# One kernel, last layer: the order of TensorE's products in the expert retrieval, the last turn of each chunk, the stores at the end, and who builds one-hots

## The chip, the cores and the metric

The kernel runs on one core of one Trainium2 chip. The metric is the device time of one execution in microseconds (us). Engines are named PE (TensorE), DVE (VectorE), ACT (ScalarE), POOL (GpSimd) and SP (SyncE).

## The reference

The network has four layers, each a gated "cross attention" and a gated feed-forward part, on x of 8 x 256 rows (2048 rows) of 512 features. The change lies in the very last part only, the fourth feed-forward:

```
q = (x @ Wq).reshape(b, t, H, 2, DK)                 # H = 4 heads
sim1, sim2 = products of the halves of q with the keys
s1, i1 = top_k(sim1, 8); s2, i2 = top_k(sim2, 8)
final_scores, pk_idx = top_k(all 64 sums, 8)         # 8 experts for each head and row
w_down, w_up = e_down[final_indices], e_up[final_indices]
hidden = silu(einsum('btd,bthkd->bthk', x, w_down)) * relu(final_scores)
out = einsum('bthk,bthkd->btd', hidden, w_up)
x = x + tanh(g_ffn[3]) * out
```

Each row has 32 chosen experts out of 4096, each with its weight. x is layer-normalised before it goes in.

## The kernel before

X stays in SBUF as 16 tiles of 128 rows. Earlier phases have left the chosen indices (`first`, `second`, transposed, and `idx`), the weights (`first[:, 1, :]`, `wts`) and the transposed x in DRAM (`xT_dram`). The phase `retrieve_phase` then does two things side by side.

Eleven tiles (TG = 11) go the dense way. They are cut into three chunks of 3, 4 and 4 tiles (NQ = 3), and for each chunk all 4096 experts are gone through in 32 blocks of 128 (EB = 32), two blocks to a turn (`k`, NP = 16 turns). Buffers come in pairs, one for an even block (h = 0) and one for an odd block (h = 1). For a block n:

- SP loads the 256 KB of down and the 256 KB of up rows. ACT rounds each to a high part (`down_high`, `up_high`), DVE takes the rest (`down_low`, `up_low`).
- `hidden` on PE (line 2610): 12 matmuls (4 pieces of the features, three products of high and low parts) give 128 experts by up to 512 rows in `h_ps[h]`.
- The chain of a block, which alternates between two engines: ACT `silu` (L2666), DVE `weight`, a product with the block of G (L2762), ACT `high` (L2671), DVE `low` (L2766).
- `add_up` on PE (line 2622): three matmuls of 512 columns for each tile of the chunk, 9 or 12, add to one accumulator `o_ps[a]` for each tile. `begin` (L2601) zeroes the accumulators, `end` (L2627) closes them.

G holds the weight of every expert for every row. It is made by products of one-hots, `weigh` on PE (L2594; 4 products, seen as 8 records): `oh2` from DVE, `oh1` from DVE (L2753) or from ACT (`one_hot`: an Abs, L2684, and a Relu, L2687, for each of the 4 columns that it takes), and ACT copies the result to G (`keep`, L2678). There are 88 groups: the first 24 (N0) are made in a loop ahead of chunk 0 (the head), where DVE alone builds the one-hots; the other 64 are made inside the turns of chunks 0 and 1, where ACT builds 3 of 4 (chunk 0) or 4 of 4 (chunk 1) of `oh1`.

PE's order in a turn of blocks n and n+1 is: hidden(n), hidden(n+1), weigh, add_up(n), weigh, add_up(n+1). Between chunks ACT rounds the next chunk's x (`xh`, L2735) and DVE takes its rest (`split_x`, L2772), after the last turn; PE waits for `xl_ready`. DVE adds the sums to X tile by tile (L2853) once `end` has closed all accumulators; `begin` of the next chunk waits for that.

Five tiles (NG = 5) go by gathering: POOL fetches for each of 160 lists of 128 rows the down and the up rows with indirect DMAs (L2554), DVE makes a dot product (L2788) and an addition (L2802) of each. These pairs are spread over the turns by `pairs_in`: 3 or 4 slots to a turn, 52, 64 and 56 to a chunk (172 in all); the addition of a list runs 12 slots behind its dot product.

All waits are semaphores, all orders are written out by hand, and every engine works strictly in its own order. At the end POOL stores the gathered tiles in one transfer (1280 KB) and the last chunk in one transfer (1024 KB).

Of the kernel before, what the change touches and what calls it, by code (L numbers as in the profile page):

```python
# [2469 lines left out]
def retrieve_phase(nc, R, A, name, xT_dram, rows_dram, first, second, idx, wts, stat, gate, out):  # L2470
# [48 lines left out]
    summed, y_ready, stored = ph.sem("summed"), ph.sem("y"), ph.sem("stored")  # L2519
# [9 lines left out]
    @block.sync  # L2529
    def _(sp):  # L2530
        def load_down(n, h):
            sp.wait_ge(edl_ready, n + 1)
            sp.dma_start(ed[h][:, :, :], A["L3_ffn_e_down"][bass.ds(n % EB, 1)].rearrange("e p c k -> p (e c) k")).then_inc(ed_in[h], 16)

        def load_up(n, h):
            sp.wait_ge(eul_ready, n + 1)
            sp.dma_start(eu[h][:, :], A["L3_ffn_e_up"][bass.ds(n % EB, 1)].rearrange("e p c -> p (e c)")).then_inc(eu_in[h], 16)

        load_up(0, 0)
        load_down(0, 0)  # L2540
        load_down(1, 1)
        load_up(1, 1)
        with sp.Fori(1, NQ * NP) as i:
            load_down(2 * i, 0)
            load_down(2 * i + 1, 1)
            load_up(2 * i, 0)
            load_up(2 * i + 1, 1)

    @block.gpsimd
    def _(pool):  # L2550
# [13 lines left out]
        for q in range(NQ):  # L2564
            for k in range(NP):
                if k == 1 and q < NQ - 1:
                    pool.wait_ge(xl_ready, DC * (q + 1))
                    pool.dma_start(xc[:, :, :], xT_dram[q + 1]).then_inc(xc_in, 16)
                if k == 2 and q:
                    pool.wait_ge(y_ready, begun[q])  # L2570
                    pool.dma_start(out[begun[q - 1] * P:begun[q] * P, :].rearrange("(a p) c -> p a c", p=P), X[:, begun[q - 1]:begun[q], :]).then_inc(stored, 16)
                for j in pairs_in[q, k]:
                    if j + ND < NU:
                        gather(rows_dram[:, :], gd, gd_in, dotted, j + ND)
                    if LAG <= j < NU + LAG - ND:
                        gather(up_rows, gu, gu_in, added, j - LAG + ND)
        pool.wait_ge(added, NU)
        pool.dma_start(out[TG * P:N, :].rearrange("(a p) c -> p a c", p=P), X[:, TG:NT, :]).then_inc(stored, 16)
        pool.wait_ge(y_ready, TG)
        pool.dma_start(out[begun[-1] * P:TG * P, :].rearrange("(a p) c -> p a c", p=P), X[:, begun[-1]:TG, :]).then_inc(stored, 16)  # L2580
# [3 lines left out]
    def _(pe):  # L2584
# [18 lines left out]
        def hidden(n, q):  # L2603
            cols = tiles[q] * P
            for h in range(2):
                pe.wait_ge(edl_ready, n + h + 3)
                pe.wait_ge(sl_ready, n + h + 1)
                for c in range(DC):
                    for m, (w, x) in enumerate(((edh, xh), (edh, xl), (edl, xh))):
                        last = pe.matmul(h_ps[h][:, 0:cols], lhsT=w[h][:, c, :], rhs=x[:, c, 0:cols],  # L2610
                                         start=(c == 0 and m == 0), stop=(c == DC - 1 and m == 2))
                last.then_inc(h_ready, 1)

        def add_up(n, q, more, late=True):
            for h in range(2):
                if more:
                    weigh(n + h + N0, h, n + h - 1 if late else None)
                pe.wait_ge(eul_ready, n + h + 3)
                pe.wait_ge(atl_ready, n + h + 3)
                for a in range(tiles[q]):  # L2620
                    for w, x in ((ath, euh), (ath, eul), (atl, euh)):
                        last = pe.matmul(o_ps[a][:, :], lhsT=w[h][:, a * P:(a + 1) * P], rhs=x[h][:, :], start=False, stop=False)  # L2622
                last.then_inc(used, 1)

        def end(q):
            for a in range(tiles[q]):
                last = pe.matmul(o_ps[a][:, :], lhsT=zero[:, :], rhs=zero[:, 0:1].to_broadcast([P, D]), start=False, stop=True)  # L2627
            last.then_inc(summed, 1)

        pe.wait_ge(zeroed, 1)  # L2630
        with pe.Fori(0, N0 // 2) as i:
            for h in range(2):
                weigh(2 * i + h, h)
        for q in range(NQ):
            pe.wait_ge(xl_ready, DC * (q + 1))
            hidden(q * EB, q)
            begin(q)
            add_up(q * EB, q, q < NQ - 1, q > 0)
            built = min(NP, max(1, (NO - N0 - q * EB) // 2))
            if built > 1:  # L2640
                with pe.Fori(1, built) as k:
                    hidden(q * EB + 2 * k, q)
                    add_up(q * EB + 2 * k, q, True)
            if built < NP:
                with pe.Fori(built, NP) as k:
                    hidden(q * EB + 2 * k, q)
                    add_up(q * EB + 2 * k, q, False)
            end(q)

    @block.scalar  # L2650
    def _(act):
# [46 lines left out]

        def turn(q, k, more):
# [8 lines left out]
            high(n + 1, 1, cols)  # L2708
            held, build = n + N0 < NO, n + N0 + 2 < NO
# [4 lines left out]
            if build:  # L2714
                one_hot(n + N0 + 2, 0, q)
# [4 lines left out]
            if build:  # L2720
                one_hot(n + N0 + 3, 1, q)
# [8 lines left out]
        down_high(1, 1)  # L2730
        for q in range(NQ):
            act.wait_ge(xc_in, 16 * q + 16)
            act.wait_ge(h_ready, q * EB + 2)
            for c in range(DC):
                act.activation(xh[:, c, 0:tiles[q] * P], xc[:, c, 0:tiles[q] * P], ACT.Copy).then_inc(xh_ready, 1)  # L2735
# [8 lines left out]
    def _(dve):  # L2744
# [65 lines left out]
        def turn(q, k, more, ahead):  # L2810
# [140 lines left out]
```

## Time and profile before

| | us |
|---|---|
| median of 3 runs | 1713.95 (1712.74 to 1713.96) |
| the profiled execution, as timed | 1718.21 |
| its span, first to last instruction | 1716.5 |
| PE busy / DVE busy / ACT busy over the span | 1370.1 / 1419.7 / 937.7 |
| the head of the retrieval (weights' loop) | about 1061 to 1105.3 |
| chunk 0, 1, 2 | 1105.3 to 1282.3, to 1502.3, to 1708.3 |

Times in rows are microseconds from the span's start. A row of the timeline has the start, the length, engine, line, operation, what is written from what is read, how many instructions are merged in it, and in brackets the idle time of the engine just before it and what ended it. Matmuls overlap one another, so their spacing is read from their starts, not from their lengths. "remote" stands where a signal ended a wait and the profile shows no instruction ending at that time; "issue" where it shows no signal.

### The profile page before, as it was taken

Reading aid. Unit: us, or ns where it says so; the run is one execution under the profiler, and the core shown is the slowest. Engines: PE = TensorE matmul, PEld = TensorE weight load, DVE = VectorE, ACT = ScalarE, POOL = GpSimd, SP = SyncE. Lnnn points to the kernel's source line nnn. Section 1 sums busy time; section 2 is a strip of 40 time slices with the busy share of each in tenths; the row PEclk is TensorE's granted clock in tenths of the full one; section 3 lists DMA queues with packets and bytes.
Section 4 is the critical chain, followed back from the end, with each engine's and each line's share of the span. In section 5 each row is a group of like instructions: output and inputs, shape, how many; then the busy total and the mean of one; then the engine's idle time right before and its main releaser. Section 6 shows DMA issues by size and latency. Waiting matters only on the chain. (4 is left out here: it accounts for less than half of the span.)

```text
span 1716.5 us, 23588 instructions
## 1 busy us (share of the span) xinstructions
PE 1370.1 (80%) x6594; PEld 1019.2 (59%) x6614; DVE 1419.7 (83%) x3057; ACT 937.7 (55%) x1967; POOL 545.1 (32%) x607
## 2 busy tenths in 40 slices
PE   3888548886999668466675981799989999989987
PEld 2444324445788533344524881699878788867766
DVE  5999868975887698798499998989888799977775
ACT  3467746652333272675434442488787788833332
POOL 0000025553110000000033224147666577746542
PEclk8899879997999866687876995999999999989999
DMA  6230020000000120464100003178887888877774
GB/s 217 92 126 13 1 80 0 0 1 1 1 1 1 46 104 1 150 206 135 56 1 19 25 26 95 49 211 256 230 240 224 229 249 241 255 208 238 220 212 143
DMA packets 92338, 197.44 MB, mean 115 GB/s; under 512 B 16040, under 2 KB 25896, under 8 KB 91488
## 3 DMA queue, kind: packets, MB, share of 16 engines
q0 software_dynamic: 27168, 90.98, 18.9%
q1 hardware_dynamic: 65088, 105.56, 18.7%
q8 instruction: 28, 0.46, 0.1%
q14 instruction: 54, 0.44, 0.1%
HBM read 181.04 MB, written 15.47 MB: 114 GB/s over the span
## 5 line engine op out<-in xcount | busy, mean ns | idle before, releaser
L2554 POOL DMA_INDIRECT L3f_gd<-rows,idx x160 | 188.5, 1178 | 192.9 <-DVE L3f_gd L2788 160.8
L2554 POOL DMA_INDIRECT L3f_gu<-in_L_ffn_e_up,idx x160 | 178.5, 1116 | 73.7 <-issue 46.3
L2622 PE MATMUL L3f_o_ps<-L3f_euh,L3f_ath 128*128 128x512 f32 x352 | 148.2, 421 | 27.1 <-DVE L3f_atl L2766 23.9
L2610 PE MATMUL L3f_h_ps<-L3f_xh,L3f_edh 128*128 128x512 f32 (+1 forms) x384 | 145.1, 378 | 9.1 <-DVE L3f_xl L2772 5.8
L2610 PE MATMUL L3f_h_ps<-L3f_xl,L3f_edh 128*128 128x512 f32 (+1 forms) x384 | 144.4, 376 | 0.0
L2610 PE MATMUL L3f_h_ps<-L3f_xh,L3f_edl 128*128 128x512 f32 (+1 forms) x384 | 144.3, 376 | 0.0
L2622 PE MATMUL L3f_o_ps<-L3f_euh,L3f_atl 128*128 128x512 f32 x352 | 140.2, 398 | 0.0
L2622 PE MATMUL L3f_o_ps<-L3f_eul,L3f_ath 128*128 128x512 f32 x352 | 139.8, 397 | 0.0
L2594 PE MATMUL L3f_g_ps<-L3f_oh 128*128 128x128 f32 x704 | 99.0, 286 | 46.4 <-DVE L3f_oh L2753 40.9
L2762 DVE TENSOR_TENSOR L3f_at<-L3f_at,L3f_G 128x512 f32<-128x512 f32 (+1 forms) x96 | 62.1, 647 | 80.3 <-ACT L3f_at L2666 51.2
L2594 PEld LDWEIGHTS L3f_g_ps<-L3f_oh 128*128 128x128 f32 x704 | 94.4, 200 | 55.0 <-issue 46.2
L2666 ACT ACTIVATE L3f_at<-L3f_h_ps 128x512 f32<-128x512 f32 (+1 forms) x96 | 53.5, 557 | 131.3 <-PE L3f_h_ps L2610 62.9
L2802 DVE SCALAR_TENSOR_TENSOR X<-L3f_gu,L3f_coef,X 128x512 f32<-128x512 f32 x160 | 119.5, 747 | 1.0
L2788 DVE SCALAR_TENSOR_TENSOR L3f_gd<-L3f_gd,L3f_xs 128x512 f32<-128x512 f32 x160 | 109.9, 687 | 0.0
L2622 PEld LDWEIGHTS L3f_o_ps<-L3f_euh,L3f_ath 128*128 128x128 f32 x352 | 67.7, 192 | 50.8 <-issue 39.1
L2687 ACT ACTIVATE L3f_oh<-L3f_oh,first,L3f_minus 128x128 f32<-128x128 f32 x216 | 90.2, 486 | 2.1
L2610 PEld LDWEIGHTS L3f_h_ps<-L3f_xh,L3f_edh 128*128 128x128 f32 x384 | 73.3, 191 | 21.1 <-DVE L3f_xl L2772 6.3
L2671 ACT ACTIVATE L3f_ath<-L3f_at 128x512 fp32r<-128x512 f32 (+1 forms) x96 | 57.4, 598 | 50.8 <-DVE L3f_at L2762 29.8
L333 PE MATMUL L0x_vp_ps<-L0x_W,L0x_V 128*128 128x512 f32 x128 | 66.8, 671 | 19.1 <-ACT L0x_sv L493 19.1
L2610 PEld LDWEIGHTS L3f_h_ps<-L3f_xl,L3f_edh 128*128 128x128 f32 x384 | 73.4, 191 | 10.9
L2610 PEld LDWEIGHTS L3f_h_ps<-L3f_xh,L3f_edl 128*128 128x128 f32 x384 | 73.2, 191 | 10.5
L1034 POOL TENSOR_TENSOR L0f_s<-L0f_s,L0f_su 128x1 f32<-128x1 f32 x16 | 5.4, 337 | 231.5 <-DVE L0f_s L1123 231.5
(595 smaller groups left out, 3755.8 us busy)
## 6 DMA issues: line engine op xcount, KB each, us to landing
L3f_eu<-in_L_ffn_e_up SPq DMA_DIRECT2D x96, 256.0 KB
L3f_ed<-in_L_ffn_e_down SPq DMA_DIRECT2D x96, 256.0 KB
L2x_ed<-in_L_ffn_e_down SPq DMA_DIRECT2D x32, 256.0 KB, 3.4
rows<-L2x_eo SPq DMA_DIRECT2D x32, 256.0 KB, 2.4
wgu<-in_L_ffn_w_gate_upT SPq DMA_DIRECT2D x4, 1408.0 KB, 7.9
X<-in_x SPq DMA_DIRECT2D x4, 1024.0 KB, 10.1
L0x_V<-in_ctxT SPq DMA_DIRECT2D x8, 512.0 KB, 3.8
L1f_C<-in_ctx SPq DMA_DIRECT2D x2, 2048.0 KB, 13.1
```

What stands on the lines that cost most here:

```text
L333: last = pe.matmul(vp_ps[:, :], lhsT=V[b % 3][:, c, j * P:(j + 1) * P], rhs=W[:, c, D:2 * D], start=(c == 0), stop=(c == DC - 1))
L1034: pool.tensor_tensor(at(s, n, 2), at(s, n, 0), at(su, n), ALU.mult).then_inc(sx_ready, 1)
L2554: pool.indirect_dma_start(buf[j % ND][:, :], None, table, bass.IndirectOffsetOnAxis(ap=idx[:, j:j + 1], axis=0)).then_inc(sem[j % ND], 16)
L2594: last = pe.matmul(g_ps[h][:, g, :], lhsT=oh2[h][:, g, :], rhs=oh1[h][:, g, :], start=True, stop=True)
L2610: last = pe.matmul(h_ps[h][:, 0:cols], lhsT=w[h][:, c, :], rhs=x[:, c, 0:cols], start=(c == 0 and m == 0), stop=(c == DC - 1 and m == 2))
L2622: last = pe.matmul(o_ps[a][:, :], lhsT=w[h][:, a * P:(a + 1) * P], rhs=x[h][:, :], start=False, stop=False)
L2666: act.activation(at[h][:, 0:cols], h_ps[h][:, 0:cols], ACT.Silu).then_inc(sl_ready, 1)
L2671: act.activation(ath[h][:, 0:cols], at[h][:, 0:cols], ACT.Copy).then_inc(ath_ready, 1)
L2687: last = act.activation(oh1[h][:, g, :], oh1[h][:, g, :], ACT.Relu, scale=minus[:, n * GR + g:n * GR + g + 1], bias=first[:, 1, n * GR + g ...
L2762: dve.tensor_tensor(ah, ah, Ge, ALU.mult).then_inc(at_ready, 1)
L2788: dve.scalar_tensor_tensor(gd[j % ND][:, :], gd[j % ND][:, :], 1.0, xs[:, j // S, :], ALU.mult, ALU.mult, accum_out=hid[:, j:j + 1]).then_ ...
L2802: dve.scalar_tensor_tensor(X[:, TG + j // S, :], gu[j % ND][:, :], coef[:, j:j + 1], X[:, TG + j // S, :], ALU.mult, ALU.add).then_inc(add ...
```

## The change

1. Products alternate. PE's order becomes hidden(n+1), weigh, add_up(n), weigh, hidden(n+2), add_up(n+1): each hidden product is issued one add_up earlier than before. hidden(n) of a chunk's first block stands ahead of the loop, and the last turn of a chunk has no hidden(n+2).
2. The split of the next chunk's x moves into the last turn: on ACT behind `high` of block n+1, on DVE behind `low` of block n+1.
3. The accumulators are closed tile by tile, each right behind the last add_up of its tile, and each closing signals; DVE's addition to X waits for its own tile only.
4. The last chunk is stored by SP, each tile when it is done; the gathered tiles are stored as 4 tiles once those are done and 1 tile at the end.
5. In the head ACT builds 1 of the 4 `oh1` of a group (from group 4 on, 22 groups), DVE 3 of 4. ACT's loop over the 24 groups is written out.

```diff
+    GH, HW = 1, 4
+    HB = N0 + 2 - HW
+    def far_before(done):
+        return HB * GH + GA[0] * min(done, EB) + GA[1] * max(done - EB, 0)
 @block.sync
+        for a in range(begun[-1], TG):
+            sp.wait_ge(y_ready, a + 1)
+            sp.dma_start(out[a * P:(a + 1) * P, :], X[:, a, :]).then_inc(out_last, 16)
+        sp.wait_ge(out_last, 16 * tiles[-1])
 @block.gpsimd
+        pool.wait_ge(added, NU - S)
+        pool.dma_start(out[TG * P:N - P, :]..., X[:, TG:NT - 1, :]).then_inc(stored, 16)
         pool.wait_ge(added, NU)
-        pool.dma_start(out[TG * P:N, :]..., X[:, TG:NT, :]).then_inc(stored, 16)
-        pool.wait_ge(y_ready, TG)
-        pool.dma_start(out[begun[-1] * P:TG * P, :]..., X[:, begun[-1]:TG, :]).then_inc(stored, 16)
+        pool.dma_start(out[N - P:N, :], X[:, NT - 1, :]).then_inc(stored, 16)
 @block.tensor
+        def add_up(n, h, q, closing=False):
...
+                if closing:
+                    pe.matmul(o_ps[a][:, :], lhsT=zero[:, :], rhs=..., start=False, stop=True).then_inc(summed, 1)
+        def turn(n, q, more, ahead=HB, first=False, last=False):
+            hidden(n + 1, 1, q)
+            if first:
+                begin(q)
+            if more:
+                weigh(n + N0, 0, ahead - 1)
+            add_up(n, 0, q)
+            if more:
+                weigh(n + 1 + N0, 1, ahead)
+            if not last:
+                hidden(n + 2, 0, q)
+            add_up(n + 1, 1, q, last)
 @block.scalar
+        def high_x(q):
+            act.wait_ge(xc_in, 16 * q + 16)
+            act.wait_ge(h_ready, q * EB + 2)
+            for c in range(DC):
+                act.activation(xh[:, c, 0:tiles[q] * P], xc[...], ACT.Copy).then_inc(xh_ready, 1)
 turn:       high(n + 1, 1, cols)
+            if k == NP - 1 and q < NQ - 1:
+                high_x(q + 1)
+                for n in range(N0):
+                    keep(n, 0, n // 2, n % 2)
+                    if n + 2 >= HW:
+                        one_hot(n + 2, n % 2, GH, GH * (n + 2 - HW))
 @block.vector
 turn:       low(n + 1, 1, cols)
+            if k == NP - 1 and q < NQ - 1:
+                split_x(q + 1)
-        with dve.Fori(2, N0 // 2 + 1) as i:
+        with dve.Fori(HW // 2, N0 // 2 + 1) as i:
             for h in range(2):
-                one_hots(2 * i + h, h)
+                one_hots(2 * i + h, h, GH)
-            if q < NQ - 1:
-                split_x(q + 1)
-            dve.wait_ge(summed, q + 1)
             for a in range(tiles[q]):
+                dve.wait_ge(summed, begun[q] + a + 1)
                 dve.scalar_tensor_tensor(X[:, begun[q] + a, :], o_ps[a][:, :], tg..., X..., ALU.mult, ALU.add).then_inc(y_ready, 1)
```

## Rows read from the trace of the kernel before

**Rows 1.** Page, part 1: busy us, share of the span, instructions of each engine.
```profile
PE 1370.1 (80%) x6594; PEld 1019.2 (59%) x6614; DVE 1419.7 (83%) x3057; ACT 937.7 (55%) x1967; POOL 545.1 (32%) x607
```
**Rows 2.** Windows over chunks 0, 1, 2: us, busy by engine, clock, DMA share, GB/s.
```profile
1105.30:1282.30 177.00, 168.31 (x935) 153.23 (x935) 158.79 (x342) 146.91 (x356) 107.72 (x88) 0.98 0.76 225
1282.30:1502.30 220.00, 210.07 (x1031) 176.79 (x1032) 191.56 (x373) 179.65 (x421) 149.20 (x133) 0.97 0.82 240
1502.30:1708.30 206.00, 188.12 (x775) 145.50 (x776) 151.58 (x288) 72.77 (x131) 99.10 (x96) 0.98 0.69 203
```
**Rows 3.** Timeline of PE, first matmuls of hidden blocks in chunks 0, 1, 2.
```profile
1116.17 0.33 PE L2610 MATMUL L3f_h_ps<-L3f_xh,L3f_edh 128*128 128x384 f32 x1
...
1126.30 0.34 PE L2610 MATMUL L3f_h_ps<-L3f_xh,L3f_edh 128*128 128x384 f32 x1
...
1304.06 0.39 PE L2610 MATMUL L3f_h_ps<-L3f_xh,L3f_edh 128*128 128x512 f32 x1
...
1306.78 0.39 PE L2610 MATMUL L3f_h_ps<-L3f_xh,L3f_edh 128*128 128x512 f32 x1
...
1316.75 0.39 PE L2610 MATMUL L3f_h_ps<-L3f_xh,L3f_edh 128*128 128x512 f32 x1
...
1520.39 0.39 PE L2610 MATMUL L3f_h_ps<-L3f_xh,L3f_edh 128*128 128x512 f32 x1
...
1695.86 0.39 PE L2610 MATMUL L3f_h_ps<-L3f_xh,L3f_edh 128*128 128x512 f32 x1
```
**Rows 4.** Windows over single turns: two of chunk 0, two of chunk 2.
```profile
1150.40:1160.60 10.20, 10.12 (x59) 9.18 (x58) 10.11 (x22) 9.00 (x23) 7.55 (x7) 1.00 0.71 230
1181.10:1192.30 11.20, 11.20 (x66) 10.41 (x65) 11.20 (x25) 9.62 (x23) 8.84 (x8) 1.00 0.84 260
...
1639.30:1651.10 11.80, 11.38 (x50) 8.84 (x49) 10.22 (x20) 4.65 (x9) 5.97 (x6) 1.00 0.82 227
1664.80:1676.70 11.90, 11.48 (x50) 8.93 (x49) 9.09 (x17) 4.73 (x10) 4.47 (x4) 1.00 0.54 163
```
**Rows 5.** Timeline of ACT and PE, waits inside chunks 1 and 2.
```profile
1349.94 0.60 ACT L2666 ACTIVATE L3f_at<-L3f_h_ps 128x512 f32<-128x512 f32 x1 [5.15 <-remote]
...
1352.80 0.77 PE L2622 MATMUL L3f_o_ps<-L3f_euh,L3f_ath 128*128 128x512 f32 x1 [4.00 <-DVE L3f_atl L2766]
...
1567.04 0.47 PE L2622 MATMUL L3f_o_ps<-L3f_euh,L3f_ath 128*128 128x512 f32 x1 [2.19 <-DVE L3f_atl L2766]
```
**Rows 6.** Timeline of DVE in the head, two groups in a row.
```profile
1102.51 0.74 DVE L2749 TENSOR_TENSOR L3f_oh<-ident,second 128x512 f32<-128x512 f32 x1
...
1103.11 1.17 DVE L2753 TENSOR_SCALAR L3f_oh<-ident,first 128x128 f32<-128x128 f32 x4
...
1104.13 0.75 DVE L2749 TENSOR_TENSOR L3f_oh<-ident,second 128x512 f32<-128x512 f32 x1
```
**Rows 7.** Timeline of ACT in chunk 1: keep, and one-hots of one group.
```profile
1297.98 0.58 ACT L2678 ACTIVATE L3f_G<-L3f_g_ps 128x512 f32<-128x512 f32 x1
...
1298.98 1.27 ACT L2684 ACTIVATE L3f_oh<-ident,first 128x128 f32<-128x128 f32 x4
1300.28 1.65 ACT L2687 ACTIVATE L3f_oh<-L3f_oh,first,L3f_minus 128x128 f32<-128x128 f32 x4
```
**Rows 8.** Timeline of PE and DVE at the two joints between chunks.
```profile
1288.06 0.80 PE L2610 MATMUL L3f_h_ps<-L3f_xh,L3f_edh 128*128 128x512 f32 x1 [5.80 <-DVE L3f_xl L2772]
...
1294.02 0.69 DVE L2762 TENSOR_TENSOR L3f_at<-L3f_at,L3f_G 128x512 f32<-128x512 f32 x1 [4.03 <-ACT L3f_at L2666]
...
1511.75 0.69 DVE L2762 TENSOR_TENSOR L3f_at<-L3f_at,L3f_G 128x512 f32<-128x512 f32 x1 [3.64 <-ACT L3f_at L2666]
```
**Rows 9.** Timeline of DVE and POOL at the end of the span.
```profile
1708.29 2.73 DVE L2853 SCALAR_TENSOR_TENSOR X<-L3f_o_ps,tg,X 128x512 f32<-128x512 f32 x4 [2.56 <-PE L3f_o_ps L2627]
...
1711.31 0.81 POOL L2580 DMA_DIRECT2D out<-X  x1 [4.36 <-DVE X L2853]
```
**Rows 10.** Page, part 6, an earlier store of 256 KB: KB, us to landing.
```profile
rows<-L2x_eo SPq DMA_DIRECT2D x32, 256.0 KB, 2.4
```

More of the change, by code:

```diff
@@ L2576, in _ @@
                         gather(up_rows, gu, gu_in, added, j - LAG + ND)
+        pool.wait_ge(added, NU - S)
+        pool.dma_start(out[TG * P:N - P, :].rearrange("(a p) c -> p a c", p=P), X[:, TG:NT - 1, :]).then_inc(stored, 16)
         pool.wait_ge(added, NU)
-        pool.dma_start(out[TG * P:N, :].rearrange("(a p) c -> p a c", p=P), X[:, TG:NT, :]).then_inc(stored, 16)
-        pool.wait_ge(y_ready, TG)
-        pool.dma_start(out[begun[-1] * P:TG * P, :].rearrange("(a p) c -> p a c", p=P), X[:, begun[-1]:TG, :]).then_inc(stored, 16)
+        pool.dma_start(out[N - P:N, :], X[:, NT - 1, :]).then_inc(stored, 16)
         pool.wait_ge(stored, 16 * (NQ + 1))
@@ L2601, in begin, with hidden @@
                 pe.matmul(o_ps[a][:, :], lhsT=zero[:, :], rhs=zero[:, 0:1].to_broadcast([P, D]), start=True, stop=False)
-        def hidden(n, q):
+        def hidden(n, h, q):
             cols = tiles[q] * P
-            for h in range(2):
[L2606 to L2633, printed above, removed]
+            pe.wait_ge(edl_ready, n + 3)
+            pe.wait_ge(sl_ready, n + 1)
+            for c in range(DC):
+                for m, (w, x) in enumerate(((edh, xh), (edh, xl), (edl, xh))):
+                    last = pe.matmul(h_ps[h][:, 0:cols], lhsT=w[h][:, c, :], rhs=x[:, c, 0:cols],
+                                     start=(c == 0 and m == 0), stop=(c == DC - 1 and m == 2))
@@ new lines, in hidden @@
+            last.then_inc(h_ready, 1)
+        def add_up(n, h, q, closing=False):
+            pe.wait_ge(eul_ready, n + 3)
+            pe.wait_ge(atl_ready, n + 3)
+            for a in range(tiles[q]):
+                for w, x in ((ath, euh), (ath, eul), (atl, euh)):
+                    last = pe.matmul(o_ps[a][:, :], lhsT=w[h][:, a * P:(a + 1) * P], rhs=x[h][:, :], start=False, stop=False)
+                if closing:
+                    pe.matmul(o_ps[a][:, :], lhsT=zero[:, :], rhs=zero[:, 0:1].to_broadcast([P, D]), start=False, stop=True).then_inc(summed, 1)
+            last.then_inc(used, 1)
@@ new lines, in turn @@
+        def turn(n, q, more, ahead=HB, first=False, last=False):
[10 more added lines that the diff above has]
+            add_up(n + 1, 1, q, last)
+        pe.wait_ge(zeroed, 1)
+        for n in range(HW):
+            weigh(n, n % 2)
@@ L2634, in _ @@
+        with pe.Fori(HW // 2, N0 // 2) as i:
+            for h in range(2):
+                weigh(2 * i + h, h, 2 * i + h - HW + 1)
         for q in range(NQ):
             pe.wait_ge(xl_ready, DC * (q + 1))
[L2636 to L2648, printed above, removed]
+            n = q * EB
+            hidden(n, 0, q)
+            turn(n, q, q < NQ - 1, n + HB if q else HB, first=True)
+            with pe.Fori(1, NP - 1) as k:
+                turn(n + 2 * k, q, q < NQ - 1, n + 2 * k + HB)
+            turn(n + 2 * NP - 2, q, q < NQ - 1, n + 2 * NP - 2 + HB, last=True)
@@ L2678, in keep, with one_hot @@
             act.activation(Gs, g_ps[h][:, :, :].rearrange("p g (a e) -> p a e g", a=4), ACT.Copy).then_inc(G_ready, 1)
-        def one_hot(n, h, q):
-            done = n - N0 - 2
+        def one_hot(n, h, given, far):
             act.wait_ge(g_ready, n + 1)
-            for g in range(GA[q]):
+            for g in range(given):
                 act.activation(oh1[h][:, g, :], io[:, :], ACT.Abs, scale=-1.0, bias=first[:, 0, n * GR + g:n * GR + g + 1]).then_inc(far_ready, 1)
-            act.wait_ge(far_ready, GA[0] * min(done + 1, EB) + GA[1] * max(done + 1 - EB, 0))
-            for g in range(GA[q]):
+            act.wait_ge(far_ready, far + given)
+            for g in range(given):
                 last = act.activation(oh1[h][:, g, :], oh1[h][:, g, :], ACT.Relu, scale=minus[:, n * GR + g:n * GR + g + 1],
@@ L2697, in hidden_units @@
                     act.activation(act_hid[:, g], hid[:, g], ACT.Silu).then_inc(hid_ready, 1)
+        def high_x(q):
+            act.wait_ge(xc_in, 16 * q + 16)
+            act.wait_ge(h_ready, q * EB + 2)
+            for c in range(DC):
+                act.activation(xh[:, c, 0:tiles[q] * P], xc[:, c, 0:tiles[q] * P], ACT.Copy).then_inc(xh_ready, 1)
         def turn(q, k, more):
@@ L2730, in _ @@
         down_high(1, 1)
+        high_x(0)
         for q in range(NQ):
[L2732 to L2735, printed above, removed]
             if q == 0:
-                with act.Fori(0, N0 // 2) as i:
-                    for h in range(2):
-                        keep(2 * i + h, 0, i, h)
+                for n in range(N0):
+                    keep(n, 0, n // 2, n % 2)
+                    if n + 2 >= HW:
+                        one_hot(n + 2, n % 2, GH, GH * (n + 2 - HW))
             for k in range(NP):
```

6 lines of the change are left out of this document (3 added, 3 removed).

## The prediction

> **What bounds the kernel now.** I read the page first, then windows, then the timeline. The page has PE at 80% and DVE at 83% of the span [rows 1]: two engines close together, so the limit has to be read stage by stage. The windows over the three chunks of the retrieval [rows 2], 603 us of 1716.5, are all that this change touches beside the head and the end. In chunk 0 PE is busy 168.3 of 177 us, DVE 158.8; in chunk 1 210.1 and 191.6 of 220; in chunk 2 188.1 and 151.6 of 206. PE's busy time counts overlapping ends, so I take its true need from starts. In chunk 0 an undisturbed turn goes from 1116.17 to 1126.30, 10.13 us; in chunk 1 from 1304.06 to 1316.75, 12.69 us, its 12 hidden matmuls taking 1306.78 - 1304.06 = 2.72 us, 0.227 each [rows 3]. A turn of chunk 2 has no `weigh`: 48 matmuls of 512 columns at 0.227 are 10.9 us. Really it takes (1695.86 - 1520.39) / 14 = 12.53 us [rows 3]. So the largest slack of PE lies in chunk 2, some 1.6 us in each turn.
>
> DVE's need: in chunk 0 it is busy for 10.11 of 10.20 us in a turn with three gathered pairs and 11.20 of 11.20 in one with four [rows 4]; with every fourth turn of the long kind that is 10.4 a turn, over PE's 10.13. Chunk 0 is bound by DVE from about its fifth turn. In chunk 2 DVE needs 10.2 or 9.1 [rows 4], mean 9.7, under PE's 10.9.
>
> What stalls PE inside the chunks is the chain silu, weight, high, low between a hidden product and its add_up. The before order leaves a block of h = 0 one hidden product (and in chunks 0 and 1 one `weigh`) of cover. The worst place shows it: ACT's silu waited 5.15 us, until 1349.94, for a signal that the profile gives to no instruction ending then ("remote"), and PE then stood 4.00 us before 1352.80 [rows 5]. PE's signal simply came late. Smaller ones of this kind cost chunk 2 about 2 us in about every second turn, as the 2.19 before 1567.04 [rows 5]. At the joints between chunks PE stands 5.80 us for the split of x, and DVE in turn 4.03 and 3.64 us for PE [rows 8].
>
> **The change part by part.** The sum is made against the profiled execution, 1718.21 us (span 1716.5 and 1.7 around it), which is 4.3 above the median of 1713.95.
>
> *Head.* DVE sets the pace, one group from 1102.51 to 1104.13, 1.62 us, of which the four tensor_scalar take 1.02 by their starts, 0.255 each [rows 6]. One of the four goes to ACT: DVE then needs 1.37. ACT needs a keep (0.58), an Abs and a Relu of one column; four of them go in 1.27 and 1.65 [rows 7], about 0.32 and 0.42 each, and a wait on its own signal between, some 1.4 together. So the period is about 1.4, ACT and DVE level, and 22 groups save 22 x 0.2 = 4.4. From both sides: 0, if the waits between ACT and PE do not overlap, to 22 x 0.25 = 5.5. I take 4; writing out the loop I cost at nothing, since ACT's instructions in the turns are written out already.
>
> *Chunk 0, alternating.* Four turns at PE's 10.13, twelve at DVE's 10.4, and 1.4 for opening and closing the accumulators make 167 of the 177 now [rows 2]. At most 10 can be won. But where DVE is the bound it lags, PE waits for add_up(n), and the extra cover is already spent: of a late signal of 3 to 4 us only part is absorbed. I take 4.5, bounds 0 and 10.
>
> *Joint 0 to 1.* The split costs DVE what it did (four subtractions, no new ones) but stands ahead of PE's last add_up instead of behind all gathers. hidden(n+2) then finds xl ready; PE waits next at `begin`, since the additions to X still stand behind a `down_low`, an `up_low`, two one-hots and three gathered pairs on DVE. DVE no longer waits its 4.03 us [rows 8], and what it does afterwards comes earlier by that. With the first turn's matmuls, which now run at the low level of the clock after the pause (the granted clock was 0.97 over the chunk [rows 2]), I take 5. *Joint 1 to 2*: 3.64 [rows 8] of DVE and about 1 of PE, 4.5. Bounds of both together: 6, if a new wait at `begin` lets the clock fall again, and 11.
>
> *Chunk 1.* At 12.69 us a turn PE has nothing left to win: alternating costs and gives nothing there. What goes is part of the one disturbance, 4.00 us and then a few us of slow matmuls (the first after it is 0.77 long, where others are 0.39 [rows 3, 5]). One more add_up of 12 matmuls, 2.7 us, stands between hidden(n) and add_up(n) now, so of the late 5.15 some 1.5 remain and the clock may stay up. I take 5, bounds 0 and 6.5.
>
> *Chunk 2, the largest term.* Cover for h = 0 grows from 2.7 to 5.4 us, and for h = 1 likewise from 2.7 (an add_up) to 5.4, against a chain of 2.86 (silu at 1349.94 to add_up at 1352.80 [rows 5]). But a new order of waits appears: hidden(n+1) now runs behind add_up(n-1), so its signal comes 5.4 us after hidden(n)'s end instead of 2.7, and `weight` of n+1 stands on DVE ahead of all gathers. Follow DVE: from `weight` of n+1 at +6.0, the remaining work of its turn (9.7 less 2.4 for weight, down_low, low and up_low) ends at +13.3, which is +2.4 in the next turn's time; `low` ends 2.1 later at +4.5; PE wants it at +5.4. So the loop closes with 1 us to spare at PE's 10.9, 0.3 in turns with four pairs. Late signals of 2 us in every second turn eat that: about 11.35 a turn. (12.53 - 11.35) x 15 = 17.7; I take 17.5. Bounds: 24 at 10.9, and 7 if only the small waits of the chain (0.2 to 0.5 us a turn) go.
>
> The same balance for chunk 1: DVE's turn of 11.7 closes its loop at 11.9, under 12.69; for chunk 0 at 10.05, under 10.4. ACT's hidden order is fine in all: high, keep and one-hots follow signals that come no later in the turn.
>
> *End.* DVE's four additions (2.73 us) end at 1711.0, POOL issues at 1711.31 [rows 9], and the span ends at 1716.5, 5.2 later. Now three of the four additions lie beside the last matmuls, the last ends about 1709.1, and a store of 256 KB on SP lands after 2.4 [rows 10]; with some 1.2 behind the landing, an estimate (5.2 less 2.4 and the longer transfer of 1024 KB), that is 1712.9. I take 3.5, bounds 1.5 and 4.7. The store of the gathered tiles is hidden by PE's last turn either way.
>
> Sum: 4 + 4.5 + 5 + 4.5 + 5 + 17.5 + 3.5 = 44. 1718.2 - 44 = 1674.2 profiled, less 4.3 for the median: **1670**.
>
> **The rivals.** *(A) Late signals stay late.* Their lateness on h = 1 goes straight into DVE, which has 1 us to spare in chunk 2 and none in chunk 0. Then chunk 0 gives 0, chunk 1 2, chunk 2 7, and with 4 + 9.5 + 3.5 the gain is 26: 1688. For it: DVE is busy in 11.20 of 11.20 us in long turns [rows 4]. Against: in chunk 2 DVE has over 1 us a turn.
>
> *(B) All is absorbed.* Head 4, chunk 0 9, joints 10, chunk 1 6, chunk 2 24, end 4 give 57: 1657. It needs signals that are late only because PE was disturbed itself.
>
> *(C) Slower.* If PE's signals come late because PE runs without a pause, the new order, which takes its pauses away, makes every signal of h = 1 late. In its place, `weight` of n+1, DVE then idles: with a delay of 2 us each turn, chunk 0 closes at 12.05 (against 11.0 now), chunk 1 at 12.9 to 13.8 (12.69), chunk 2 at 12.85 (12.53). That costs 17 + 13 + 5 = 35 against 17.5 from joints, head and end: 1731. It decides from about 1.2 us of delay in every turn. For it: late signals stand in stages of full PE. Against: chunk 1 took 220 us [rows 2], which is 16 turns at 12.69 (203), one such disturbance and the joint, so most of its turns, though PE never pauses in them, have none.
>
> *(D) The clock falls.* The granted clock is 0.97 or 0.98 in all three chunks [rows 2]. If PE, waiting briefly for DVE in more places, ran at 0.90, its 570 us of matmuls would grow by 8%, 45 us, and eat the gain: 1715. The Trainium skill, "TensorE: Matmul & The Clock Gate", section "A second HAM failure mode: psum-queue depth-cycling", says that a PE that pauses often and briefly between groups, as it moves from one accumulator bank to the next, can swing between its two clock levels. That speaks against finer alternation; the trace disagrees so far, with 1.00 in four single turns that have such pauses and bank changes [rows 4], so by the page the time would be this rival's, by the rows the forecast's.
>
> *(E) Nothing changes*, because DVE goes through its work in the old order and PE's new order only moves its waits: the joints, the head and the end would still be there, so this is (A) at least. Only if the early hidden(n+2) waited for `down_low` would it not do what it says; DVE does that second in its turn, some 6 us before.
>
> **How the numbers follow.** Forecast 0.60 (1662 to 1680), A 0.20, B 0.10, C 0.05, D and others 0.05. A comparison of this kernel can tell about 0.2%, 3.4 us. Faster 0.92, within 0.2% 0.02, slower 0.06. The range: the sum of upper bounds (5.5 + 10 + 11 + 6.5 + 24 + 4.7 = 62) ends at 1652, which needs all at once, so 1655; above, A with 4 us on it, 1692.
>
> **What would show it.** PE's hidden starts in chunk 2 about 11.3 us apart, no bracket over 1 us before L2622 in most turns; chunk 1 at 12.69 as before; no wait for L2772 at the joints, one of 1 to 3 us at `begin`; a head period of 1.4 us; the last store issued near 2 us after PE's last matmul. The prediction is wrong if chunk 2's turn stays above 12, or if chunk 1's leaves 12.69, or if DVE shows waits for silu before `weight` of the odd block that add up to more than it lost before.

## The result and the profile after

The changed kernel took 1673.67 us in the median (1671.16 to 1676.94) beside 1713.35 us for the kernel before: a ratio of 0.9775, 95% interval 0.9752 to 0.9798. The forecast was 1670 in 1655 to 1692. The profiled execution took 1676.94 us with a span of 1675.2; against 1716.5 the span is 41.3 us shorter. These runs, with the kernel before's, are called the first measurement below.

The windows over the three chunks of the changed kernel, in the columns of [rows 2] (us, busy by engine, clock, DMA share, GB/s):

```profile
1101.90:1273.20 171.30, 165.76 (x936) 151.27 (x937) 158.17 (x339) 147.62 (x356) 107.58 (x87) 1.00 0.77 232
1273.20:1483.40 210.20, 207.02 (x1032) 174.28 (x1033) 192.26 (x374) 178.01 (x423) 145.73 (x131) 0.99 0.85 251
1483.40:1671.90 188.50, 180.26 (x775) 144.55 (x774) 152.30 (x289) 73.63 (x131) 102.27 (x99) 0.99 0.77 228
```

Each chunk is shorter (177.0, 220.0 and 206.0 before), DVE is as busy in each as before to within 0.8 us, and the granted clock rose from 0.97 or 0.98 to 0.99 or 1.00. In the kernel before, six stretches of 3.4 or 6.8 us inside this time ran at a granted clock of 0.5, the level of 1.2 GHz, each at or just behind a pause of PE; in the changed kernel two of 3.4 us are left, at 1281.1 and 1540.6. Two windows of the kernel before, in the same columns:

```profile
1286.00:1292.80 6.80, 4.74 (x11) 3.77 (x12) 3.99 (x7) 0.06 (x1) 2.87 (x3) 0.50 0.66 196
1350.90:1357.70 6.80, 4.90 (x12) 3.88 (x13) 6.67 (x13) 5.57 (x14) 2.36 (x2) 0.50 0.67 184
```

For the sums below I cut the time at PE's own events, the same in every trace: the head (first `weigh` to first hidden), chunk 0 (to its last closing), joint (from there to the next chunk's first add_up), and so on. In us, both profiled in the first measurement:

| | before | after | won | forecast |
|---|---|---|---|---|
| ahead of the head | 1061.1 | 1059.4 | 1.7 | 0 |
| head | 44.3 | 42.5 | 1.8 | 4 |
| chunk 0 | 176.9 | 171.3 | 5.6 | 4.5 |
| joint 0 to 1 | 15.3 | 11.3 | 4.0 | 5 |
| chunk 1 | 204.6 | 198.9 | 5.7 | 5 |
| joint 1 to 2 | 12.3 | 7.3 | 5.0 | 4.5 |
| chunk 2 | 193.8 | 181.3 | 12.5 | 17.5 |
| end | 8.2 | 3.3 | 4.9 | 3.5 |

PE's starts of hidden blocks in the changed kernel, one and the same place of a turn in each pair, answer to [rows 3]:

```profile
1114.86 0.33 PE L2620 MATMUL L3f_h_ps<-L3f_xh,L3f_edh 128*128 128x384 f32 x1
1124.99 0.33 PE L2620 MATMUL L3f_h_ps<-L3f_xh,L3f_edh 128*128 128x384 f32 x1
...
1293.69 0.39 PE L2620 MATMUL L3f_h_ps<-L3f_xh,L3f_edh 128*128 128x512 f32 x1
1306.38 0.39 PE L2620 MATMUL L3f_h_ps<-L3f_xh,L3f_edh 128*128 128x512 f32 x1
...
1498.91 0.39 PE L2620 MATMUL L3f_h_ps<-L3f_xh,L3f_edh 128*128 128x512 f32 x1
...
1651.28 0.39 PE L2620 MATMUL L3f_h_ps<-L3f_xh,L3f_edh 128*128 128x512 f32 x1
```

An undisturbed turn is 10.13 us in chunk 0 and 12.69 in chunk 1, as before: PE's own work has not changed. Chunk 2's turn is (1651.28 - 1498.91) / 13 = 11.72 us, where it was 12.53. What it still loses has a second cause. SP's, ACT's and PE's timeline in the changed kernel:

```profile
1514.38 0.33 SPq L2540 DMA_DIRECT2D L3f_ed<-in_L_ffn_e_down  x1
...
1522.10 0.63 ACT L2668 ACTIVATE L3f_edh<-L3f_ed 128x512 fp32r<-128x512 f32 x1 [3.14 <-DMA L3f_ed<-in_L_ffn_e_down]
...
1539.87 0.47 PE L2629 MATMUL L3f_o_ps<-L3f_euh,L3f_ath 128*128 128x512 f32 x1 [4.50 <-DVE L3f_atl L2783]
```

ACT waits for down rows that are on their way. The kernel before had one wait of 0.6 us of this kind in chunk 0 and none in chunk 2. The stall of 4.50 us itself has both causes. The hidden product of the block in question (number 72 of 96, counted from 0) had its last matmul at 1529.54, but its silu began only at 1535.72:

```profile
1529.54 0.39 PE L2620 MATMUL L3f_h_ps<-L3f_xh,L3f_edl 128*128 128x512 f32 x1
...
1535.72 0.60 ACT L2678 ACTIVATE L3f_at<-L3f_h_ps 128x512 f32<-128x512 f32 x1 [5.96 <-PE L3f_h_ps L2620]
```

The bracket names PE because the next block's hidden product happened to end then; this is a late signal of 5.8 us. `high` then stood behind another wait for down rows, of 1.45 us.

At joint 0 to 1 the wait for the split is gone and PE stands at `begin`; DVE goes from its last addition straight to `weight`, where it had waited 4.03 us [rows 8]:

```profile
1280.40 0.74 DVE L2870 SCALAR_TENSOR_TENSOR X<-L3f_o_ps,tg,X 128x512 f32<-128x512 f32 x1
1281.06 0.69 DVE L2779 TENSOR_TENSOR L3f_at<-L3f_at,L3f_G 128x512 f32<-128x512 f32 x1
...
1281.21 0.61 PE L2612 MATMUL L3f_o_ps<-identb 128*128 128x512 bf16 x1 [2.56 <-DVE X L2870]
```

At the end the last addition is alone behind PE and the four stores follow one another on SP; the span ends at 1675.2, 2.5 us after that addition. Against [rows 9]:

```profile
1670.01 3.03 SPq L2557 DMA_DIRECT2D out<-X  x4
...
1671.93 0.75 DVE L2870 SCALAR_TENSOR_TENSOR X<-L3f_o_ps,tg,X 128x512 f32<-128x512 f32 x1 [0.18 <-PE L3f_o_ps L2631]
```

In the head DVE's groups are not all alike. One takes 1.62 us as in [rows 6], because DVE waits 0.16 for PE's `weigh`, the next 1.38:

```profile
1090.27 0.69 DVE L2766 TENSOR_TENSOR L3f_oh<-ident,second 128x512 f32<-128x512 f32 x1
1090.87 0.86 DVE L2770 TENSOR_SCALAR L3f_oh<-ident,first 128x128 f32<-128x128 f32 x3
1091.89 0.69 DVE L2766 TENSOR_TENSOR L3f_oh<-ident,second 128x512 f32<-128x512 f32 x1 [0.16 <-PE L3f_g_ps L2605]
1092.50 0.85 DVE L2770 TENSOR_SCALAR L3f_oh<-ident,first 128x128 f32<-128x128 f32 x3
1093.27 0.69 DVE L2766 TENSOR_TENSOR L3f_oh<-ident,second 128x512 f32<-128x512 f32 x1
```

### The profile page after: what moved, and what is told of

It is laid out like the page before. It is cut to its first block and busy times, and to the rows that moved or that the text cites. A ratio compares the mean times of both kernels' runs of the same rounds, so it can differ in the third digit from the quotient of the medians.

```text
span 1675.2 us, 23554 instructions
## 1 busy us (share of the span) xinstructions
PE 1353.9 (81%) x6594; PEld 1012.3 (60%) x6614; DVE 1414.4 (84%) x3035; ACT 953.4 (57%) x2011; POOL 543.1 (32%) x607
## 5 line engine op out<-in xcount | busy, mean ns | idle before, releaser
L2565 POOL DMA_INDIRECT L3f_gd<-rows,idx x160 | 182.8, 1142 | 164.5 <-DVE L3f_gd L2805 133.8
L2629 PE MATMUL L3f_o_ps<-L3f_euh,L3f_ath 128*128 128x512 f32 x352 | 143.2, 407 | 14.3 <-DVE L3f_atl L2783 9.2
L2698 ACT ACTIVATE L3f_oh<-L3f_oh,first,L3f_minus 128x128 f32<-128x128 f32 x238 | 101.2, 487 | 2.8
L2779 DVE TENSOR_TENSOR L3f_at<-L3f_at,L3f_G 128x512 f32<-128x512 f32 (+1 forms) x96 | 62.0, 645 | 42.5 <-ACT L3f_at L2678 26.1
L2620 PEld LDWEIGHTS L3f_h_ps<-L3f_xh,L3f_edh 128*128 128x128 f32 x384 | 72.3, 188 | 10.1
L2620 PEld LDWEIGHTS L3f_h_ps<-L3f_xl,L3f_edh 128*128 128x128 f32 x384 | 72.2, 188 | 10.1
```

The lines of the kernel that those rows point to most:

```text
L2565: pool.indirect_dma_start(buf[j % ND][:, :], None, table, bass.IndirectOffsetOnAxis(ap=idx[:, j:j + 1], axis=0)).then_inc(sem[j % ND], 16)
L2698: last = act.activation(oh1[h][:, g, :], oh1[h][:, g, :], ACT.Relu, scale=minus[:, n * GR + g:n * GR + g + 1], bias=first[:, 1, n * GR + g ...
L2779: dve.tensor_tensor(ah, ah, Ge, ALU.mult).then_inc(at_ready, 1)
```

## The experiments

They ran on three chips: the four single parts on one, `after_again`, `before_again`, `both` and `light_after` on a second, `chain_first`, `best` and `light_before` on a third. The number of the first measurement's chip is not known. Every ratio is to the kernel before on the chip of that run. Stage times below are from one profiled execution each, cut as in the table above.

**One part at a time.** `alt_only` is the kernel before with only the new order of products:

```diff
-            for h in range(2): hidden(n + h, h, q)      # both hidden products first
+            hidden(n, 0, q)                             # ahead of the chunk's first turn only
+        turn: hidden(n + 1, 1, q); weigh; add_up(n, 0, q); weigh; hidden(n + 2, 0, q); add_up(n + 1, 1, q)
```

> The kernel before with the alternating order of products alone: split of x, closing, stores and head as before. Theory (the order gives a late signal more cover): it keeps the gains of chunk 0, of chunk 1's one disturbance and of chunk 2, which the changed kernel's trace has at 5.7, 5.7 and 12.5 us, so 24 less than before, about 1690, ratio 0.986; chunk 2's turn about 11.2 us. Rival 1 (the order only pays when the joints are out of the way, because PE enters each chunk late otherwise): 8 to 12 us at most. Rival 2 (PE's order does nothing, DVE sets everything): within 3 us of before.

Measured: 1680.82 us, ratio 0.9965 (0.9944 to 0.9986). Chunk 0 166.9, chunk 1 197.9, chunk 2 177.7. The 24 us of the theory are not there; 0.35% is 6 us, between the two rivals. Nearly all of it lies in chunk 2, which takes 183 us in the three kernels of the old order beside it. This miss is the most telling of the runs, because those three explain it. `no_alt` is the changed kernel with the old order:

```diff
+            hidden(n, 0, q)
             hidden(n + 1, 1, q)
...
-            if not last:
-                hidden(n + 2, 0, q)
```

> The changed kernel with PE's order of products put back (hidden n, hidden n+1, then the two add_ups); split in the last turn, closing by tile, stores and head as changed. Theory: the gain that is left is joints 9, end 4.9, head 2 to 3, together 16 to 17: about 1697, ratio 0.990; chunk 2's turns back at 12.5 us. Rival 1 (the parts hang together): under 10 us are left. Rival 2 (the order does nothing): 38 us are left, 1674.

Measured: 1671.91 us, ratio 0.9908 (0.9874 to 0.9942); 15.7 us less than before by the medians, as the theory had it, but with the kernel before at 1687.57 us, not at 1713. Chunk 0 168.2, chunk 1 198.6, chunk 2 183.3 us.

`split_only` moves only the split of x:

```diff
 turn (ACT): high(n + 1, 1, cols)
+            if k == NP - 1 and q < NQ - 1: high_x(q + 1)
 turn (DVE): low(n + 1, 1, cols)
+            if k == NP - 1 and q < NQ - 1: split_x(q + 1)
```

> The kernel before with the split of the next chunk's x in the last turn alone. Theory: PE no longer waits for the split (5.80 and 3.31 us before), but waits at begin for DVE's additions; DVE loses its 4.03 and 3.64 us of waiting. Gain 8 to 9, 1705, ratio 0.995. Rival (the wait only moves to begin): 0 to 3 us. The trace should show the time from the last closing to the first add_up of the next chunk: 15.3 and 12.3 us before, 11.3 and 7.2 in the changed kernel.

Measured: 1678.58 us, ratio 0.9949 (0.9924 to 0.9974). The joints are 11.3 and 7.4 us, within 0.1 us what the changed kernel has in the first measurement. The wait for the split (5.80 before) is replaced by one of 2.60 us at `begin`:

```profile
1277.76 1.89 PE L2608 MATMUL L3f_o_ps<-identb 128*128 128x512 bf16 x4 [2.60 <-DVE X L2863]
```

`end_only` has only the closing by tile and the stores:

```diff
-        end(q)                                # one signal for all accumulators
+        closing of tile a right behind its last add_up, with its own signal
-        POOL: out[last chunk] in one transfer
+        SP: out[tile a] when y_ready reaches a + 1
```

> The kernel before with closing by tile and the new stores alone. Theory: 8.2 us from the last closing to the end of the span before become 3.3, as in the changed kernel's trace; gain 4.9, ratio 0.997. Rival (the closings between the add_ups and the four stores cost what they give): 0 to 1.5 us.

Measured: 1680.31 us, ratio 0.9962 (0.9944 to 0.9979), end 3.3 us instead of 8.2. The median is 7.3 us lower, the stage 4.9; I take the stage, which is inside the interval.

In `split_only` and `end_only` chunks 0 to 2, in the old order, take 167.5, 198 and 183 us; in the first measurement the same order took 176.9, 204.6 and 193.8. In none of these four traces does a wait in the retrieval end in "remote". In the first measurement seven did in the kernel before on one line alone, in the changed one five (line, what was waited for: us in total, times, longest):

```profile
ACT L3f_at L2666 <- remote: 22.3, 7, 7.3
```
```profile
ACT L3f_at L2678 <- remote: 10.9, 5, 3.6
```

The two traces of the first measurement lack some of the signals' records (12279 and 12109 of them, against 15353 to 15917 in the eleven others), so this reading needs a second one that does without them. From the instructions' own times: with ACT idle, silu began over 0.8 us after its hidden product's end for eight blocks of the kernel before (up to 4.9 us) and six of the changed one (up to 5.8), and for none in any of the eleven later traces. Blocks 67, 72, 79, 83 and 87 are late in both kernels. From ACT to DVE, from DVE to ACT and from DVE to PE nothing in the chain is late in any trace.

So the kernel alone does not make the late signals. They belong to the first measurement, to its chip or to its moment (no run separates the two), where they fall on the same places of the program in both kernels. Most of what the three chunks won there belongs to it too.

**The same kernels without late signals.** A chip whose runs show no late signal is called quiet below. `after_again` and `before_again` are the two kernels unchanged.

> The changed kernel itself, unchanged, for its time and trace beside kernels of the same chip. On the chip of the four runs before this, where no wait of the retrieval ended in a signal without an instruction, the kernel before took 1687.6 and the changed one without the alternation 1671.9. Theory (alternation pays by the disturbances that it covers): where they are missing, the changed kernel is 22 us under before, 1666, ratio 0.987, chunk 2 near 177 us between its first add_up and last closing; where they are there, ratio 0.977 and chunk 2 over 180. Rival (the chips differ in something else, and the ratio is a property of the change): 0.977 anywhere.

> The kernel before, unchanged, for its trace on the same chip as the three beside it. On a chip without late signals: chunk 0 167.5 us, chunk 1 198, chunk 2 183; on one with them 177, 205, 194.

Measured: 1666.08 us, ratio 0.9863 (0.9841 to 0.9885), against 1666 and 0.987 expected; before_again 1689.05 us, with chunks of 167.8, 198.9 and 183.0 us. The interval lies clear of 0.9775: the ratio is no property of the change alone. The changed kernel's chunks are 167.9, 200.0 and 176.6. So on a quiet chip the alternation gives nothing in chunks 0 and 1, and 6.4 us in chunk 2; joints, head and end give the rest (joints 5.9 and 3.9, head 1.9, end 4.9).

**What chunk 2 is made of.** Two kernels leave out work: their loads in chunk 2 bring 8 of 128 partitions.

```diff
+        for a, b, p in ((1, 2 * NP, P), (2 * NP, NQ * NP, 8)):
+            with sp.Fori(a, b) as i: load_down(2 * i, 0, p) ... load_up(2 * i + 1, 1, p)
```

> The changed kernel whose loads of down and up rows in chunk 2 bring 8 of 128 partitions (16 KB in place of 256 KB each), so that the other partitions keep old rows. Theory (what is left over 10.9 us a turn in chunk 2 is loads that land late, ACT waited 3.14, 1.17 and 1.45 us for them, and the traffic behind them): chunk 2 takes 16 x 10.9 + 1, 175 to 176 us in place of 181, with no bracket over 1 us before an add_up. Rival (DVE's four pairs in a turn and late signals do it): 179 or more.

> The kernel before whose loads of down and up rows in chunk 2 bring 8 of 128 partitions (16 KB in place of 256 KB), the others keeping old rows. It tells what the old order costs with no late load: with the changed order and light loads chunk 2 was 170.4 us, PE's own need. Theory (without late loads the old order still loses the chain's 0.2 to 0.5 us at both add_ups of a turn, for its cover of 2.7 us against a chain of 2.8): 178 to 179 us, against 183.0 with full loads on the same kind of chip. Rival (all of the old order's loss is late transfers): 171 to 172.

Measured, one execution each: light_after 1662.6 us, chunk 2 170.4 and no stall in it; light_before 1689.3 us, chunk 2 183.0, as with full loads. Hidden starts 14 turns apart in chunk 2, for before_again, light_before, after_again and light_after in this order:

```profile
1501.98 0.39 PE L2610 MATMUL L3f_h_ps<-L3f_xh,L3f_edh 128*128 128x512 f32 x1
...
1666.73 0.39 PE L2610 MATMUL L3f_h_ps<-L3f_xh,L3f_edh 128*128 128x512 f32 x1
```
```profile
1502.18 0.39 PE L2611 MATMUL L3f_h_ps<-L3f_xh,L3f_edh 128*128 128x512 f32 x1
...
1666.91 0.39 PE L2611 MATMUL L3f_h_ps<-L3f_xh,L3f_edh 128*128 128x512 f32 x1
```
```profile
1487.33 0.39 PE L2620 MATMUL L3f_h_ps<-L3f_xh,L3f_edh 128*128 128x512 f32 x1
...
1645.92 0.39 PE L2620 MATMUL L3f_h_ps<-L3f_xh,L3f_edh 128*128 128x512 f32 x1
```
```profile
1489.97 0.39 PE L2621 MATMUL L3f_h_ps<-L3f_xh,L3f_edh 128*128 128x512 f32 x1
...
1642.40 0.39 PE L2621 MATMUL L3f_h_ps<-L3f_xh,L3f_edh 128*128 128x512 f32 x1
```

A turn takes 11.77, 11.77, 11.33 and 10.89 us. The old order loses 0.88 us a turn to the chain's lack of cover, and its loads, late or not, cost it nothing that shows; both guesses beforehand (178 to 179, 171 to 172) were wrong, since the cover's lack was dearer than I had read from the brackets. An add_up of before_again shows it:

```profile
1542.68 0.39 PE L2610 MATMUL L3f_h_ps<-L3f_xh,L3f_edl 128*128 128x512 f32 x1
1543.29 0.47 PE L2622 MATMUL L3f_o_ps<-L3f_euh,L3f_ath 128*128 128x512 f32 x1 [0.22 <-DVE L3f_atl L2766]
1543.60 0.40 PE L2622 MATMUL L3f_o_ps<-L3f_eul,L3f_ath 128*128 128x512 f32 x1
```

The bracket says 0.22, but the two steps between starts are 0.61 and 0.31 where undisturbed ones are 0.227: 0.47 us lost, twice a turn.

The new order takes the 0.88 away, PE then runs at its own need, and loads that had time enough in the old order give back 0.44. From the third turn of chunk 2 on, ACT in before_again was ready for the down rows of an even block 8.1 us after their issue (median), in after_again 5.8 us, and they take 3.7 and 4.8 us to land in the median but up to 8.4 and 11.3. This is the longest wait of ACT for one in after_again, a load issued 11.3 us before ACT could use it:

```profile
1518.53 0.68 SPq L2540 DMA_DIRECT2D L3f_ed<-in_L_ffn_e_down  x1
...
1529.84 0.63 ACT L2668 ACTIVATE L3f_edh<-L3f_ed 128x512 fp32r<-128x512 f32 x1 [6.33 <-DMA L3f_ed<-in_L_ffn_e_down]
...
1531.94 0.47 PE L2629 MATMUL L3f_o_ps<-L3f_euh,L3f_ath 128*128 128x512 f32 x1 [3.63 <-DVE L3f_atl L2783]
```

**Moving work out of the bound stage.** `both` evens out DVE's load and moves its additions at the joints:

```diff
-            c = (3 + (k % 4 == 3), 4, 4 - k % 2)[q]
+            c = (3, 4, 4 - (k % 4 == 1))[q]
 last turn of chunks 0 and 1 (DVE): additions to X
+            gathered(pairs_in[q, NP - 1][2:])        # behind them, not ahead
```

> The changed kernel with two edits: at the joints DVE adds the chunk's sums to X ahead of the last two or three gathered pairs of the turn, so that begin waits less; and one gathered pair in four turns moves from chunk 0 to chunk 2 (3 a turn, 4, 3.75 in place of 3.25, 4, 3.5). Theory: PE's wait at begin (2.56 us and slow matmuls behind it at joint 0 to 1, 0.94 at joint 1 to 2) goes, 4 us; DVE has 4 pairs of 1.28 us less in chunk 0, where it is the bound, 5 us less, and still room in chunk 2 at 10.1 of 10.9 us: 0 to 2 lost. Together 5 to 8 us under the changed kernel. Rival 1 (chunk 2 is bound by transfers, and pairs moved there lengthen it): 0 to 3. Rival 2 (the wait at begin only moves to add_up, for DVE's chain of the first block): gain of the joints under 1.

Measured: 1666.5 us, ratio 0.9862 (0.9840 to 0.9884), the changed kernel's own time; the 5 to 8 us did not come. Chunk 0 fell from 167.9 to 164.2 and joint 0 to 1 from 9.9 to 8.8; chunk 1 rose from 200.0 to 201.9, chunk 2 from 176.6 to 183.8 and the end from 3.3 to 4.4. DVE's bound in chunk 0 is real, but chunk 2 grew by 7.2 us with the pairs. DVE's own work does not explain it: it is busy for 150.5 of the 185.1 us from 1477.9 to 1663.0. ACT's waits for down rows grew, from 12.7 to 23.3 us in sum over chunk 2, as the first rival has it; whether the added gathers or a chance of this one trace made the loads later was not separated. Its worst stall, with ACT's wait ahead of it:

```profile
1551.87 0.63 ACT L2668 ACTIVATE L3f_edh<-L3f_ed 128x512 fp32r<-128x512 f32 x1 [8.46 <-DMA L3f_ed<-in_L_ffn_e_down]
...
1553.97 0.77 PE L2629 MATMUL L3f_o_ps<-L3f_euh,L3f_ath 128*128 128x512 f32 x1 [5.76 <-DVE L3f_atl L2783]
```

**A late load out of the chain's way.** `chain_first`, in chunk 2 only (one gathered pair of DVE moves too, into the place that `down_low` leaves):

```diff
 ACT: silu(n, 0, cols)
-     down_high(n + 2, 0)
      high(n, 0, cols)
+     down_high(n + 2, 0)
 DVE: weight(n, q, k, 0)
-     down_low(n + 2, 0)
+     gathered(js[:1])
      low(n, 0, cols)
+     down_low(n + 2, 0)
```

> The changed kernel where, in chunk 2 alone, ACT rounds the next down rows behind `high` of the block at hand instead of ahead of it, and DVE takes their rest behind `low` (a gathered pair fills its place). In the changed kernel's trace on the calm chip ACT waited 6.33 us for down rows that landed 11.3 us after their issue, with `high` queued behind, and PE stood 3.63 us. Theory (the one stall left in chunk 2 is this queue place): hidden(n+2) is due one add_up later than add_up(n), so 2.7 us and more of lateness cost nothing; chunk 2 goes from 176.6 to 172 or 173, the time from 1666.1 to about 1662, ratio 0.984. Rival (the transfers are late in any case and PE then waits at hidden(n+2) for the same): no change in chunk 2, 176 to 177.

Measured: 1662.24 us, ratio 0.9852 (0.9829 to 0.9875), chunk 2 171.8 us. The hidden starts 14 turns apart:

```profile
1490.00 0.39 PE L2620 MATMUL L3f_h_ps<-L3f_xh,L3f_edh 128*128 128x512 f32 x1
...
1643.81 0.39 PE L2620 MATMUL L3f_h_ps<-L3f_xh,L3f_edh 128*128 128x512 f32 x1
```

10.99 us a turn against 11.33, and ACT still waits for loads (up to 4.3 us at a time): they are late as before, but `high` no longer stands behind them. The stage shows it (176.6 and, in alt_only, 177.7 with the old place); the whole kernel's interval overlaps the changed kernel's.

`best` adds two edits:

```diff
+ last turn of chunks 0 and 1 (DVE): the last gathered pairs behind the additions to X, as in `both`
-            load_down(2 * i, 0); load_down(2 * i + 1, 1); load_up(2 * i, 0); load_up(2 * i + 1, 1)
+            load_down(2 * i, 0); load_up(2 * i - 1, 1); load_down(2 * i + 1, 1); load_up(2 * i, 0)
```

> The kernel of chain_first, with DVE's additions to X ahead of the last gathered pairs at the joints, and SP's loads in the order in which their buffers come free (down n+4, up n+3, down n+5, up n+4), which issues each even down load some 1.2 us earlier. Theory: chain_first's gain, 1.1 us at joint 0 to 1 (9.9 to 8.8, as measured with both edits before), and fewer late loads in chunks 1 and 2: 1660, ratio 0.983. Rival: the loads' order changes nothing and only chain_first's gain and 1 us are seen.

Measured: 1661.65 us, ratio 0.9842 (0.9823 to 0.9862). Chunk 1 199.3 (chain_first 200.8), chunk 2 174.0 (171.8), joint 0 to 1 10.1 us in both: neither edit shows over chain_first, though the loads of even blocks in chunk 2 now are issued 8.4 us ahead of ACT in the median instead of 6.7. A chunk's time varies by 2 to 3 us from trace to trace where the code is the same (chunk 1: 200.0 in after_again, 203.3 in light_after), so of the place's worth in chunk 2, 2.6 us (best) to 4.8 (chain_first) can be said. Where `begin` does not wait, the first add_up does:

```profile
1277.10 0.76 PE L2633 MATMUL L3f_o_ps<-L3f_euh,L3f_ath 128*128 128x512 f32 x1 [2.69 <-DVE L3f_atl L2789]
```

Both kernels have lower medians than the changed kernel on its quiet chip (1666.08), by 4 us, about what can be told. They did not run beside it on one chip.

## Why the prediction was right, point by point

The forecast of 1670 was near, and the bounds and the mechanism were read rightly for the first measurement. Luck has a part in it: chunk 2 gave 5 us and the head 2.2 us less than forecast, while the two other chunks, the end and the time ahead of the head gave 4.9 us more in sum. And the 44 us hold for that measurement alone: on a quiet chip the change is worth 22.6 us (1688.65 - 1666.08), half of it.

*The bounds.* Right for each chunk: PE at 12.69 us a turn in chunk 1 has nothing to win, and did not win there without disturbances (198.9 before, 200.0 after); DVE bounds chunk 0 (taking four pairs from it shortened it by 3.7 us); PE's need in chunk 2 is 10.9 (10.89 measured once nothing disturbs it).

*Chunk 2, the mis-sized term.* 17.5 us were forecast, 12.5 measured. The mechanism was right and larger than its stated part: "only the small waits of the chain (0.2 to 0.5 us a turn)" was 0.88 in truth, while the late signals, put at 2 us in every second turn, cost 10.8 us in all (193.8 against 183.0). The brackets before an add_up understate the small waits, because a matmul's shown length overlaps the next start; the starts' spacing tells them. What failed is the price of the rest. I had only late signals as what eats the gain, and loads were not weighed at all, though a change that moves hidden(n+2) and the chain up asks how early their loads are issued: ACT was ready for them 2.3 us sooner after their issue. On the quiet chip that took back 0.44 us a turn. In the first measurement, where the loads' wait and late signals come together (11.72 a turn against 10.89), their shares cannot be split.

*The late signals.* "PE's signal simply came late" fits the instructions' times, and the extra cover absorbed about what was said: 5.6 us in chunk 0, of the 9.1 by which it was longer than on a quiet chip, and 5.7 in chunk 1; nothing is won in either without late signals. But I priced it as the kernel's property. The three chunks together gave 23.8 us in the first measurement, where the alternation was not run by itself, and on a quiet chip 6.4 in chunk 2 and nothing in the others; joints, head and end give about 16 in either place (15.7 and 16.6). Rival C, late signals because PE runs without a pause, is refuted by the quiet chips: PE runs denser there, and no signal is late. Rival A's 1688 and rival B's 1657 lie on either side of what the first measurement gave: B fell short for the loads and for late signals that stayed, A because most late signals were absorbed. What makes PE's signal late, or whether the matmuls themselves ended later than the trace's estimate, stays open.

*Joints.* 4.0 and 5.0 for 5 and 4.5. The new wait at `begin` is where it was placed, 2.56 us for "1 to 3", and the slow matmuls behind it are there: the four zeroings take 1.89 us. Whether they come hangs on little: behind 2.60 us in split_only they take 1.89 too, behind 2.40 in after_again 1.04, with no fall of the granted clock, and the joint is 9.9 us instead of 11.3.

*Head.* 1.8 for 4; on a quiet chip 1.9 (42.5 to 40.6). The period was put at 1.4 us; it is 1.5 in the mean, 1.62 and 1.38 in turn in the trace above and 1.45 to 1.55 in after_again. In the trace above DVE finds its buffer still held by PE's `weigh` every second time. The term took DVE and ACT level and left out the way round through PE.

*End.* 4.9 for 3.5: the time behind the last addition is 2.5 us in all (1672.7 to 1675.2), not 2.4 and another 1.2.

*The clock.* Rival D, after the Trainium skill's "TensorE: Matmul & The Clock Gate", section "A second HAM failure mode: psum-queue depth-cycling", did not come: the granted clock rose to 0.99 and 1.00. But the new order is no harder test of what the page describes. A turn of chunk 2 has ten changes of bank in either order, and PE's pauses became fewer: eleven steps of over 1 us between starts inside the chunks before, seven after. In this kernel the alternation took pauses away rather than adding them.

## What to carry to other kernels

Read a stage's loss from the spacing of starts against a turn that nothing disturbs, and price the cover of a chain in that currency. When a stage speeds up, list the transfers that must now land earlier and what is queued behind the instruction that waits for them: moving that instruction behind the critical chain was worth 2.6 to 4.8 us of the 6.2 that late loads cost (176.6 against 170.4), without making any transfer faster. Before a gain is put down to an edit, measure both kernels a second time, on another chip: here some three quarters of what the chunks won (23.8 us against 6.4) hung on the first measurement.

## What the runs showed of the hardware that was not expected

In the first measurement PE's signal reached ACT up to 5.8 us after the hidden product's end by the trace, in two different kernels and at the same blocks, and the kernel before took 25 to 26 us longer than on the three chips of the later runs (1713.35 against 1687.57, 1688.65 and 1687.72). Why is open; no later run met it again. A load of 256 KB among indirect gathers, in stages of 228 and 234 GB/s, became usable 7.7 and 11.3 us after its issue. Most take less: in after_again the down rows land after 4.8 us in the median, 8.2 or less for nine in ten, 12.6 at the longest.
